# Between the halves of an attention and expert kernel: row loads ahead of weight loads, one expert's low parts on VectorE, the last output base behind the scatters

## What is computed

```python
h = _layernorm(x) * (1 + ca) + sa
x = x + ga * _L0_attn_ref(h, ...)   # a causal scan, then a gated feed-forward net, as residuals
h = _layernorm(x) * (1 + cb) + sb
x = x + gb * _L0_ffn_ref(h, ...)

def _L0_ffn_ref(x, router_w, w1, v1, w2, bias):      # E = 8 experts, TOP_K = 2, F = 704
    scores = softmax(xt @ router_w)
    expert_weights, expert_idx = top_k(scores, TOP_K)
    h = gelu(xt @ w1[e]) * (xt @ v1[e])
    y = h @ w2[e]
    out = sum(expert_weights * y[of the two chosen]) + bias
```

## Time and profile before

| | us |
|---|---|
| median of three runs | 918.5 |
| lowest and highest | 917.31, 919.8 |
| the profiled execution | 916.48 |
| its span | 914.7 |
| TensorE busy | 823.5 (90% of the span) |
| DVE, ACT, POOL busy | 578.7, 370.3, 445.7 |

### The profile page before, as it was taken

The page is one execution under the profiler, slowest core; times in us unless marked ns, Lnnn a source line. Parts: engine busy times, 40 slices in busy tenths (PEclk is TensorE's granted clock), DMA queues, the critical chain, the costliest instruction groups (busy, mean ns, idle before and its releaser), DMA issues.

```text
span 914.7 us, 19914 instructions
## 1 busy us (share of the span) xinstructions
PE 823.5 (90%) x5017; PEld 730.6 (80%) x5018; DVE 578.7 (63%) x1636; ACT 370.3 (40%) x672; POOL 445.7 (49%) x444
## 2 busy tenths in 40 slices
PE   6799999999999985019999999999999999999994
PEld 2588898898989874018998988989989898999993
DVE  6668777888758565504666565566665756655553
ACT  4775666657474332103233242342432434232221
POOL 1344655968668685822345344343343533433433
PEclk9799999999999986559999999999999999999998
DMA  7111050211302314362224224242252222222221
GB/s 266 36 47 47 2 167 24 94 63 55 93 3 94 95 34 147 128 219 55 46 35 132 47 35 132 45 132 36 38 141 35 35 43 39 35 39 42 35 47 17
DMA packets 49207, 65.31 MB, mean 71 GB/s; under 512 B 4944, under 2 KB 43984, under 8 KB 49168
## 3 DMA queue, kind: packets, MB, share of 16 engines
q1 hardware_dynamic: 35200, 46.03, 17.5%
q0 software_dynamic: 13392, 18.27, 9.9%
q10 hardware_dynamic: 576, 0.54, 0.2%
HBM read 41.28 MB, written 23.54 MB: 71 GB/s over the span
## 4 chain that ended last, share of the span: by engine, by line
PE 83%; POOL 5%; DMA 3%; DVE 3%; issue 2%; ACT 2%; SPq 1%; DVEq 0%; ACTq 0%; POOLq 0%
PE ps L1379 13%; PE ps L1381 13%; PE ps L1380 13%; PE ps L466 10%; PE ps L468 10%; PE ps L467 10%; PE ps L1412 5%; DMA out_rows<-y_moe,tok_moe 2%; POOL routed L1248 2%; PE ps L1388 2%; PE ps L558 1%; PE ps L1427 1%; PE ps L1426 1%; POOL w_moe_lo L371 1%; PE ps L515 1%
## 5 line engine op out<-in xcount | busy, mean ns | idle before, releaser
L1565 POOL TENSOR_TENSOR y_moe<-y_moe 128x256 f32<-128x256 f32 x71 | 51.9, 731 | 245.1 <-DVE y_moe L1529 245.1
L1379 PE MATMUL ps<-w_moe_hi,xT_moe_hi 128*128 x426 | 167.4, 393 | 1.4 <-DVE xT_moe_lo L1511 1.4
L1381 PE MATMUL ps<-w_moe_lo,xT_moe_hi 128*128 x426 | 161.4, 379 | 0.0
L1380 PE MATMUL ps<-w_moe_hi,xT_moe_lo 128*128 x426 | 161.1, 378 | 0.0
L1571 POOL DMA_INDIRECT out_rows<-y_moe,tok_moe x71 | 111.2, 1566 | 33.9 <-issue 33.4
L1470 ACT ACTIVATE hidT_hi<-ps 128x768 fp32r<-128x768 f32 x71 | 57.9, 815 | 163.8 <-PE ps L1412 163.8
L1464 ACT ACTIVATE gelu_moe<-ps 128x704 f32<-128x704 f32 x71 | 54.0, 760 | 133.8 <-PE ps L1381 133.8
L1379 PE MATMUL ps<-w_moe_hi,hidT_hi 128*128 x355 | 105.8, 298 | 2.3 <-issue 2.3
L1381 PE MATMUL ps<-w_moe_lo,hidT_hi 128*128 x355 | 100.3, 283 | 0.0
L1380 PE MATMUL ps<-w_moe_hi,hidT_lo 128*128 x355 | 99.9, 281 | 0.0
L1529 DVE SCALAR_TENSOR_TENSOR y_moe<-ps,gate_moe,gates 128x256 f32<-128x256 f32 x142 | 62.1, 479 | 51.8 <-PE ps L1427 45.8
(11 more groups left out here) (195 smaller groups left out, 1973.5 us busy)
## 6 DMA issues: line engine op xcount, KB each, us to landing
raw<-in_w SPq DMA_DIRECT2D x8, 1408.0 KB
x_moe<-routed SPq DMA_DIRECT2D x74, 132.5 KB, 2.2
raw<-in_w SPq DMA_DIRECT2D x8, 640.0 KB
x_sb<-in_x SPq DMA_DIRECT2D x8, 512.0 KB, 3.7
x_again<-in_x SPq DMA_DIRECT2D x8, 512.0 KB
out_rows<-x_again SPq DMA_DIRECT2D x8, 512.0 KB
gu_raw<-in_gu_t SPq DMA_DIRECT2D x1, 1536.0 KB, 7.3
out_rows<-y_moe,tok_moe POOLq DMA_INDIRECT x71, 4.2
```

The costliest lines, as they stand in the source:

```text
L1379: pe.matmul(dst, a_hi, b_hi, start=first, stop=False)
L1380: pe.matmul(dst, a_lo, b_hi, start=False, stop=False)
L1381: return pe.matmul(dst, a_hi, b_lo, start=False, stop=last)
```

## The change

It moves instructions between the halves; no arithmetic is added or left out.

- On SP, the load of expert 2 goes from ahead of the pads to behind four row loads of the second half. The store of the last output base (block 7) goes there too, just ahead of it, and the load of expert 3 from behind the second row load to behind the sixth. SP no longer waits for the last base between the halves.
- On DVE, both pieces of expert 0's w1 and v1 and its w2 are split at `r == 9`; the piece at `r == 10` is gone. The split of expert 1 gets a wait for all output bases (`base_r`). The first tile gets a wait for all stores of bases (`base_out`) at its end.
- On POOL, `result_base(7)` goes from between the scatters of block 6 to behind those of block 7. The split of expert 0's w2 is DVE's now, that of expert 1's w2 goes behind the first tile's addition to the output, which waits for `base_out`.

```diff
                 if r == NBLK + 2:
                     sp.wait_ge(out_mm, NBLK * 2)
                     load_expert(sp, 1, 1)
-                if on(r - 3):
+                if on(r - 3) and r - 3 < NBLK - 1:
                     store_base(r - 3)
...
-            load_weights(sp, 1, 2, 0)
             pad_experts(sp, range(0, E, 2))
-            sp.wait_ge(base_out, NBLK * 16)
             sp.wait_ge(pads_out, E * 16)
...
-                if r == 10:
-                    split_w13_lo(v, 0, 0, pieces=[1])
...
                 if r == 9:
-                    split_w13_lo(v, 0, 0, pieces=[0])
+                    split_w13_lo(v, 0, 0)
+                    split_w2_lo(v, 0, 0)
...
             v.tensor_copy(tab[0:TAB_N, :], tp[0][0:TAB_N, 0:P]).then_inc(tab_ready, 1)
+            v.wait_ge(base_r, NBLK)
             split_w13_lo(v, 1, EXPW)
...
-                if on(r - 3):
+                if on(r - 3) and r - 3 < NBLK - 1:
                     result_base(r - 3)
...
             for r in range(-1, 12):
                 step(r)
-            for e in range(2):
-                split_w2_lo(g, e, e * EXPW)
+            result_base(NBLK - 1)
...
-            for n in range(SLOTS + ALONE - 1):
+            for n in range(SLOTS):
                 load_rows(Tile(n))
-                if n == 1:
-                    load_weights(sp, 2, 3, 1)
+            sp.wait_ge(base_r, NBLK)
+            sp.dma_start(out[(NBLK // 2 - 1) * BLK + S:NBLK // 2 * BLK + S, :]
+                         .rearrange("(i p) d -> p i d", p=P), x_again[:, (NBLK - 1) % 2]).then_inc(base_out, 16)
+            load_weights(sp, 1, 2, 0)
+            for n in range(SLOTS, SLOTS + ALONE - 1):
+                load_rows(Tile(n))
+            load_weights(sp, 2, 3, 1)
...
                 take_gates(t.near(1))
+                v.wait_ge(base_out, NBLK * 16)
...
+            def first(t):
+                g.wait_ge(base_out, NBLK * 16)
+                add_rows(t)
+                split_w2_lo(g, 1, EXPW)
+
...
-            tiles(g, add_rows, step, lambda t: None)
+            tiles(g, first, step, lambda t: None)
```

## The result

The changed kernel takes **909.09 us** (median, 907.83 to 910.65 in four runs) against 919.15 (917.31 to 920.06) for the kernel before in the same group: a ratio of 0.9893, 95% interval 0.9875 to 0.9911. That is faster by 10.1 us. The forecast was 904.0, with a range to 908.5: right in sign, wrong by 5 us in size, and the median lies 0.6 us outside the range. Of the 5.1 us, 0.65 is the starting point: I subtracted from 918.5, and the kernel before stands at 919.15 here. As a gain it is 10.1 where 14.5 was forecast. The profiled execution took 908.07, with a span of 906.3 against 914.7.

The account below looks back on a forecast made before the run. The change touches only the hole between attention blocks and expert tiles, where TensorE idles behind a chain of waits. Gains of 12.4 after the last scatter and 2.15 before it sum to 14.5: 918.5 to 904.0 us, range 900.5 to 908.5.

Parts of the forecast that it names:

- The tie with DVE: After the last scatter: row load path and DVE's path over block 7's base both take 6.25 us; 0.2 added.
- Behind the first tile: Expert stage: POOL's late split of expert 1's w2 delays expert 3's load, with six us of slack; cost nothing.
- (b): Before the last scatter: the other half of w13 no longer stretches a scatter to 2.18; gain 1.22 us.
- (c): Before the last scatter: expert 1's split no longer runs under the scatters; gain 1.95 us.
- fourth rival: Between the halves: pads land later, in one crowd with scatters; four us more gives gain 10.5, time 908; chance 7%.
- rival 1: Before the last scatter: POOL gets in after DVE's first split, up to 3.27 earlier; 900.7, likelier 901 to 903; 15%.
- (d): Before the last scatter: block 7's base leaves the run of scatters; gain 2.25 us.
- Term (a): Before the last scatter: DVE's three splits of expert 0 block POOL's mark of block 6 until 365.50; cost 3.27 us.
- The forecast's own sign for this: POOL's mark of block 6: the forecast is wrong if it ends at 362.2.
- The second sign: Row loads of the expert half: the forecast is wrong if one is issued later than 390.
- the third: Expert tiles: the forecast is wrong if TensorE waits for rows of a tile 5 to 8.
- Rival 3: Before the last scatter: the two stretched scatters were not DVE's doing, so 3.2 us stay lost; 907.2; chance 5%.

Follow-up runs that it names:

- gates first: The changed kernel plus one wait: POOL's late split of expert 1's w2 waits for VectorE's gate columns of the third tile; ratios 0.9807, 0.9838, 0.9814.
- e5_after_again: The changed kernel, unaltered, timed again on another chip; 909.43 us against 918.39 for the kernel before.
- e9_before_traced: The kernel before, unaltered, traced on the same chip as the changed kernel and gates first; 917.39 us.
- e6_late_w2: e2_sp_order_only with POOL's split of expert 1's w2 moved behind the first tile's scatter-add; 911.46 us against 918.39 for the kernel before.
- e7_base_back: gates first with the output base of block 7 put back into the run of scatters; 907.76 us against 918.39 for the kernel before.
- e8_splits_later: gates first with VectorE's three splits of expert 0 moved behind the table of tiles; 905.15 us against 918.39 for the kernel before.
- e12_gates_and_pads: gates first with all eight pad stores issued by ScalarE, none by SyncE; 906.37 us, ratio 0.9878 to the kernel before.
- e13_pads_late: gates first with SyncE and ScalarE waiting for all scatters to land before issuing the pads; 904.96 us against 915.11 for the kernel before.
- e16_base_back_again: The kernel of e7_base_back timed again, beside gates first on one chip; 902.42 us, ratio 0.9857 to the kernel before.
- e11_gates_again: gates first timed again, beside the changed kernel on one chip; 901.98 us, ratio 0.9838 to the kernel before.
- e15_gates_third: gates first timed a third time, as base of the last group; 897.83 us, ratio 0.9814 to the kernel before.
- e14_order_only_again: The kernel of e2_sp_order_only timed again, beside gates first on one chip; 901.29 us, ratio 0.9848 to the kernel before.
- e2_sp_order_only: The kernel before with only SyncE's new order of pads and weight loads; 900.56 us, ratio 0.9841 to the kernel before.
- e3_pads_on_scalar: The changed kernel with all eight pad stores issued by ScalarE, none by SyncE; 901.79 us, ratio 0.9842 to the kernel before.
- e1_gates_first: The first timing of gates first; 898.08 us at 915.98 for the kernel before, ratio 0.9807.

## Why the prediction was wrong

**The order on SyncE was right, and nearly to the tenth.** On the chip without a crawl, gates first has xT_lo at 3.02 + 3.32 = 6.34 us behind the last scatter; the forecast said 6.5 against 18.9. The scatter's landing, bounded between 1.4 and 2.6 and taken as 2.0, is 382.72 - 380.95 = 1.77 in the chain shown above. SP's part behind it, taken as 0.8, is 1.25: the same register steps as before, with 0.44 ahead of the last of them (at 383.44) where the kernel before had 0.04. The row load took 2.06. The tie with DVE fell by 0.2 to the row load: xT_lo waits for ACT, not for DVE.

**"Behind the first tile" is the step that failed.** It said of POOL's split behind the first scatter-add: "Six us of slack; nothing." That was the slack of expert 3's load. I had asked who waits for the split, and not who stands beside it. DVE's gate product was held for 4.46 us and the path lost 4.5. It is larger than any other term that was missed, and it was not even among the rivals. The trace of before has no row for it: POOL's two w2 splits there lie where DVE is idle, so nothing in it showed the two engines' SBUF work side by side in this direction, and the cost was put at nothing all the same. The section of the Trainium skill that I weighed against terms (b) and (c), page SBUF — State Buffer, section Who interferes with whom, also says that a VectorE instruction with two SBUF inputs contends with a GpSimd instruction that reads SBUF; the runs bear that out, with 4.46 against 0.16, and I had read it for one direction only. What was said of expert 3's load itself held: behind the first tile TensorE waits for no tile's rows in the trace of the changed kernel.

**The pads were covered in the forecast and are not on every chip.** Its fourth rival had the right object, pads that land late; the cause it gave, DMAs in a crowd, is not the one seen. What is slow is the issue: register steps of 0.70 us on SP and ACT, in step with each other, PE and DVE touched now and then, POOL not. It cost 1.8 us in group 3 (4.84 instead of 3.03) and 2.6 in the first trace and in `e5_after_again`. In five traces the last slow step ended within 0.3 us of the end of POOL's base of block 7, for instance 388.54 and 388.60 in `e5_after_again`. But on the chip of groups 1 and 4 the same kernels have none. The kernel before issued only ScalarE's four pads beside the scatters, and they took 4.80 and 4.07 in `e9_before_traced`, at about their usual pace. Nor is it the chip alone: on the chip of `e5_after_again` SP's four pads took 13.23 there, 7.90 and 7.94 in `e6_late_w2` and `e7_base_back` and 5.17 in `e8_splits_later`, where DVE's splits held a scatter over the pads for 3.21, 3.19 and 4.53. Together with `e12_gates_and_pads` this suggests that the slow steps need POOL's writing of scatters or its base beside them; the run that would test it, `e13_pads_late`, fell on the chip without a crawl. The cause stays open.

**Before the last scatter, rival 1 was right, with the caught scatter that it allows for.** The forecast was 2.15 earlier, with 3.27 of loss for a mark blocked until all three splits were through. The mark took 1.50; two scatters were stretched by 1.27 and 0.33 instead; the last scatter came 3.9 earlier. Of the sum, (b), (c) and (d) hold: their 5.42 less these stretches (1.27 + 0.33, less 0.08 of the 1.04 that already stood there) is the 3.9 measured. With the base put back, (c) and (d) return as 4.5 us in `e7_base_back` (5.3 in `e16_base_back_again`, where the scatter under the pair took 4.01) against the 4.2 written down. Term (a) was mis-sized: 1.52 instead of 3.27, and that is the 1.75 between 2.15 and 3.9. The forecast's own sign for this came true: the mark ended at 364.64 in a trace whose last residual was 2.42 later, that is at 362.22. The second sign, a row load issued later than 390, came at 392.11, which less the same 2.42 is 389.69; the third, a wait for rows, did not come.

**Rival 3 falls.** The stretched scatters are DVE's doing. In the changed kernel all eight pads lie beside scatters of 0.96 to 0.99, and in `e8_splits_later` the stretch follows the splits. Here the trace and what the Trainium skill, page SBUF — State Buffer, section Who interferes with whom, infers (descriptor writing needs the write side, which such a tensor_tensor doesn't take) remain at odds: a scatter of 0.96 takes 4.53 beside DVE's tensor_tensor with two SBUF inputs. In the other direction nothing was held: the gate product beside the scatter-add took 0.16.

**The sum, with the measured sizes.** On one chip (group 3): the forecast's 14.5, plus 1.75 for the earlier last scatter, less 4.6 for the stall, less 1.8 for the crawl, is 9.9; the traces have 11.3. Of the 1.4 left, the stretch from xT_lo to the end has it (3.15 longer, not 4.6). In gates first that stretch is 506.23 against 507.76 of before on the same chip. Most of the difference lies in two tiles, 7.50 and 7.22 us from gelu to gelu in `e9_before_traced` (the 22nd and the 39th) and 6.77 and 6.84 in `e11_gates_again`, with VectorE waiting 1.8 and 1.5 us for a scatter-add to land in the one and 0.9 and 0.6 in the other; 0.7 lies behind the last gelu. What sets the two tiles wasn't tested. In groups 1 and 4 gates first has 508.2 to 508.4, and that is the clock: 0.8 us more in the first tile, where it stays at half until about 6.5 us behind xT_lo in `e15_gates_third` and 4.5 in `e11_gates_again`, and 1.2 to 1.4 more behind the last gelu. There TensorE stands idle for 2.33 us in every one of these traces, and in `e15_gates_third` its products behind that run at half clock,

```profile
881.80:885.20 3.40, 3.40 (x17) 3.17 (x15) 0.11 (x2) 0.00 (x0) 0.83 (x1) 0.50 0.35 39
```

where 17 of them take 2.02 at a granted clock of 1.00 in `e11_gates_again`.

Without the stall, gates first gains 917.39 - 901.98 = 15.4 on a chip that crawls, and 915.11 - 897.83 = 17.3 on one that doesn't. That lies in the 901 to 903 of rival 1 (918.5 - 17.3 = 901.2), with a scatter caught by the next split as it says. That it comes so near to the rival's full 17.8 is in part luck: the last scatter came 1.75 earlier than forecast, not 3.27, and about 1 us of the 17.3 is in no term of the sum.

**Which version is best.** Gates first has ratios to the kernel before of 0.9807, 0.9838 and 0.9814 in its three groups. The changed kernel stood beside it in one of them, at 0.9888; in its other groups it had 0.9893 and 0.9904. Most of it is SyncE's order (0.9841 and 0.9848 alone). Expert 0's low parts on VectorE in one run bring nothing that could be measured: they take 3.4 us from POOL behind the scatters, which spares the first tile's gate product its 1.58 us, and hand 1.6 or more back in stretched scatters.

## What to carry to other kernels

When an instruction is moved off the critical path, look at what stands beside it at its new place, not only at what waits for it: a long two-input pass over SBUF on GpSimd held VectorE's smallest two-input product for its whole length here, and a short wait that kept them apart gave all of it back. Look at one engine's in-order queue first, since there a call that waits for something slow, with urgent work behind it, is the cheapest thing to repair; here it was most of the gain (15.4 of 17.9 us in group 1). And a price of nothing needs a row as much as any other.

## What the runs showed of the hardware that was not expected

- POOL's split of 4.1 us held a VectorE product of 128x1 with both inputs in SBUF for 4.42 to 4.47 us (0.16 otherwise); a product that began while a split ran was held for 1.58 and 1.59, until the split ended (`e14_order_only_again`, `e2_sp_order_only`). VectorE work with an input in PSUM went on beside it at 0.88.
- A scatter beside VectorE's splits took between 1.28 and 4.53 us instead of 0.96. At block 6 POOL got in behind the first and again behind the second split in the traces with the run of three there (mark 1.50, scatters 2.23 and 1.28 or 1.29); behind the table it got in only after the last (2.91, 3.19, 3.21, 3.50, 4.01, 4.53). Each stretched scatter ended 0.83 to 0.91 us behind the end of a split, nearly the 0.96 that one takes alone, as if it had begun there. Which of the two happens wasn't settled.
- TensorE's idle time of 2.8 us at the third tile was followed by 3.4 us near 1.2 GHz in the changed kernel (granted clock 0.56) and by no drop in `e3_pads_on_scalar` (1.00). The same stall cost 4.5 us in the one and 3.0 in the other. The idle time of 2.33 us in the last tile was followed by 3.4 us at half clock in `e1_gates_first`, `e3_pads_on_scalar`, `e7_base_back` and `e15_gates_third`, and by full clock for these products in `e11_gates_again`.
- Register and issuing steps of 0.70 us on SyncE and ScalarE together, for up to 13 us, while POOL wrote scatters and its last base. There were none in the eight traces of one chip; on the others they ran from a single one (`e8_splits_later`) to most steps of the pads.
- The attention half, with the same code, took 346.3 to 353.6 us up to its last residual: 346.3 to 347.9 in the eight traces of one chip, 350.2 to 353.6 in the eight of two others. Two kernels timed on different chips can't be compared to better than some 5 us by their traces; their ratios to the kernel before on the same chip are better, and the same chip for both is best.
